# A graph layer beside a normalised node stream: forty node tiles moved from the counting stage to the segment sums

## The reference

```python
edge_index = jnp.stack([src, dst])                    # row = src, col = dst
neighbor_sum = segment_sum(x[col], row, n)            # layer 0
deg = maximum(segment_sum(1, row, n), 1)
mean_neighbor = neighbor_sum / deg
h_mean = (x + mean_neighbor) * 0.5 @ W_mean + b_mean
h_concat = [x @ W_ego + b_ego, mean_neighbor @ W_nb + b_nb]
gate = sigmoid(gate_weight * node_vec + gate_bias)
x = layernorm(x + (1 - gate) * h_mean + gate * h_concat)
...
h = per head: softmax-like weights of edges from two-layer features, segment sums over row   # layer 1
x = layernorm(x + h)
```

## Time and profile before

| | us |
|---|---|
| median of 3 runs (lowest, highest) | 3582.08 (3581.09, 3584.49) |
| the profiled execution, its own time | 3585.29 |
| its span, first to last instruction | 3583.2 |
| mean granted TensorE clock over the span | 0.965 |

### The profile page before, as it was taken

One profiled execution on the slowest core, in us unless ns is written; L12 is line 12 of the kernel. 1 busy time (PEld: TensorE's weight loads), 2 busy tenths in 40 slices (PEclk: granted clock), 3 DMA queues, 4 the chain that ended last, 5 costly groups with the idle time before them and its releaser, 6 DMA issues. The chain is left out here.

```text
span 3583.2 us, 66785 instructions
## 1 busy us (share of the span) xinstructions
PE 3161.0 (88%) x15901; PEld 2177.7 (61%) x15901; DVE 2730.8 (76%) x9307; ACT 1892.2 (53%) x4499; POOL 1802.4 (50%) x1831
## 2 busy tenths in 40 slices
PE   4998887885898888499999999999999999995775
PEld 2455555553555555377777777777777777773333
DVE  4999997875333334388888888888888888887997
ACT  3666666663555545244444444444444444443886
POOL 0006675665777775544444444444444444420777
PEclk9999999997999999799999999999999999997998
DMA  4988777863555555433333333333333333322885
GB/s 146 322 312 274 259 259 266 276 214 123 184 170 177 177 183 183 136 124 117 117 117 117 117 116 115 116 115 116 115 115 116 116 116 116 116 80 78 270 270 196
DMA packets 289120, 596.12 MB, mean 166 GB/s; under 512 B 41438, under 2 KB 198922, under 8 KB 289062
## 3 DMA queue, kind: packets, MB, share of 16 engines
q1 hardware_dynamic: 212950, 362.51, 30.1%
q0 software_dynamic: 75744, 232.45, 20.0%
q10 hardware_dynamic: 368, 0.52, 0.0%
HBM read 287.39 MB, written 322.05 MB: 170 GB/s over the span
## 5 line engine op out<-in xcount | busy, mean ns | idle before, releaser
L1027 PE MATMUL bank<-w_node,xT 128*128 128x384 f32 x1564 | 605.5, 511 | 95.3 <-ACT bank L615 94.2
L1216 POOL TENSOR_TENSOR u_hc<-u_hc 128x1536 f32<-128x1536 f32 x98 | 270.2, 2758 | 759.5 <-DVE u_h L1326 735.4
L1438 PE MATMUL bank<-xh,w1h 128*128 128x512 f32 x1568 | 538.8, 425 | 19.1 <-DVE xl L1355 14.3
L1268 ACT ACTIVATE hidT<-bank,b1c 128x512 f32<-128x512 f32 x392 | 268.6, 685 | 536.3 <-PE bank L1438 536.2
L1438 PE MATMUL bank<-xh,w1l 128*128 128x512 f32 x1568 | 495.0, 397 | 0.0
L1438 PE MATMUL bank<-xl,w1h 128*128 128x512 f32 x1568 | 491.8, 395 | 0.0
L1349 DVE TENSOR_SCALAR hidT<-bank,b1c 128x512 f32<-128x512 f32 x392 | 294.3, 751 | 202.9 <-PE bank L1438 199.8
L1027 PEld LDWEIGHTS bank<-w_node,xT 128*128 128x128 f32 x1564 | 287.3, 198 | 264.8 <-ACT bank L615 118.8
L1452 PE MATMUL bank<-hidT,w2f 128*64 128x256 f32 x3136 | 381.7, 385 | 1.5 <-issue 1.5
L615 ACT ACTIVATE bank<-bias_all 128x512 f32<-128x512 f32 x391 | 235.0, 601 | 273.1 <-DVE H L725 267.8
L1364 DVE STREAM_TRANSPOSE feat<-catT 32x256 f32<-32x256 f32 x784 | 342.8, 437 | 17.1 <-ACT catT L1277 3.0
(11 more groups left out here) (273 smaller groups left out, 6612.9 us busy)
## 6 DMA issues: line engine op xcount, KB each, us to landing
hc_tab<-H SPq DMA_DIRECT2D x78, 960.0 KB
hc_tab<-zero_row SPq DMA_DIRECT2D x26, 2880.0 KB
er<-edge_tab SPq DMA_DIRECT2D x98, 512.0 KB, 4.4
X<-in_x SPq DMA_DIRECT2D x78, 640.0 KB
out_x<-O SPq DMA_DIRECT2D x78, 640.0 KB
edge_tab<-u_x SPq DMA_DIRECT2D x98, 256.0 KB, 2.2
edge_tab<-feat SPq DMA_DIRECT2D x98, 256.0 KB, 2.2
u_hc<-hc_tab,u_idx POOLq DMA_INDIRECT x392, 4.3
```

The costliest lines, as they stand in the source:

```text
L1027: ins = t_.matmul(p[:, 0:384], xT[i % XR][:, c * P:(c + 1) * P], w_node[:, c, :], start=False, stop=c == 1, skip_group_check=True)
L1216: g.tensor_tensor(c, c, u_hc[s][:, :, MULT:MULT + 3].unsqueeze(3).to_broadcast([P, 4, 3, P]), ALU.mult).then_inc(u_scaled, 1)
L1268: a.activation(hidT[m][:, :], bank[2 + m % 2][:, :], ACT.Relu, bias=b1c[:, m:m + 1])\
L1438: ins = t_.matmul(bank[2 + m % 2][:, :], w[:, c, m * P:(m + 1) * P], xx[s][:, c, :], start=n == 0, stop=n == 5)
```

## The change

Counting handles 48 edge tiles in a round of ten node tiles, and the segment sums handle 16, where both handled 24. Counting so ends 40 node tiles earlier, everything up to the sums moves forward by 40 tiles, and the sums take 40 node tiles more. With it: the one-hot ring is 12 deep instead of 8 in use, `RS` is 16, one PSUM bank holds the transposes of the sums and four hold their products (two and three before), a semaphore counts the gathers of two neighbouring buffers, and the clears are 15 of 26 node tiles instead of 26 of 15.

```diff
-        e_idx = sb("e_idx", [P, 24, 4], I32)
+        e_idx = sb("e_idx", [P, 32, 4], I32)
-        ZT = 15
+        ZT = 26
-        oh = tmp("oh", [P, TEN, 2 * DIG], F16)
+        CR = 12
+        oh = tmp("oh", [P, CR, 2 * DIG], F16)
-        RS = 12
+        RS = 16
-        xg_in = [sem(f"xg_in{q}") for q in range(RS)]
-        cn_out = [sem(f"cn_out{q}") for q in range(RS)]
+        xg_in = [sem(f"xg_in{q}") for q in range(RS // 2)]
+        cn_out = [sem(f"cn_out{q}") for q in range(RS // 2)]
-        CNT, FIRST, SORT1, SORT2, TABLES, SUMS, FIX = 0, 83, 85, 189, 291, 293, 378
-        AT = [0, 2, 4, 7, 9, 12, 14, 16, 19, 21]
-        TURNS, PRODS = (3, 4), (5, 6, 7)
-        LOOPS = ((2, 8), (10, 18), (20, 28), (30, 37))
+        CNT, FIRST, SORT1, SORT2, TABLES, SUMS, FIX = 0, 43, 45, 149, 251, 253, 379
+        PER = {CNT: 4 * CR, SUMS: RS}
+        AT = {begin: [many * w // TEN for w in range(TEN + 1)] for begin, many in PER.items()}
+        TURN, PRODS = 3, (4, 5, 6, 7)
+        LOOPS = ((2, 4), (6, 14), (16, 24), (27, 37))
-        def tiles24(j, i, begin, late=0):
+        def tiles_of(j, i, begin, late=0):
             r, w = run(j, i, begin + late)
-            for k in range(AT[w], AT[w + 1] if w + 1 < TEN else 24):
-                t = r * 24 + k
+            for k in range(AT[begin][w], AT[begin][w + 1]):
+                t = r * PER[begin] + k
...
                     if after(t, 2 * RS):
-                        for r in range(RS):
-                            pool.wait_ge(cn_out[r], (n * 2 + q // RS - 1) * 16)
+                        for r in range(RS // 2):
+                            pool.wait_ge(cn_out[r], (n * 2 + q // RS - 1) * 32)
...
                 def run_sum(t, q, n):
-                    dve.wait_ge(xg_in[q], n * 16 + 16)
+                    dve.wait_ge(xg_in[q // 2], n * 32 + 32)
...
                 def turn_sum(t, q):
                     pe.wait_ge(acc_ready, t + 1)
-                    if after(t, 2):
-                        pe.wait_ge(turned_out, t - 1)
+                    if after(t, 1):
+                        pe.wait_ge(turned_out, t)
...
                 def product_sum(t, q):
                     pe.wait_ge(turned_out, t + 1)
-                    if after(t, 3):
-                        pe.wait_ge(cn_ready, t - 2)
+                    if after(t, 4):
+                        pe.wait_ge(cn_ready, t - 3)
```

More of the change, by code:

```diff
@@ L587, in put @@
                                          in_=cn[q % RS][:, :], in_offset=None, bounds_check=last_half, oob_is_err=False)\
-                        .then_inc(cn_out[q % RS], 16)
+                        .then_inc(cn_out[q % RS // 2], 16)
                 ringed(pool, ET, 2 * RS, [(put, 10), (index, 0), (fetch, 0)])
-                for q in range(RS):
-                    pool.wait_ge(cn_out[q], SLOTS[q] * 16)
+                for r in range(RS // 2):
+                    pool.wait_ge(cn_out[r], (SLOTS[2 * r] + SLOTS[2 * r + 1]) * 16)
                 g.dma_start(head_c[:, :], hc_tab[N:N + P, 0, :]).then_inc(head_in, 16)
@@ L642, in copy_sum @@
                         act.wait_ge(prod_ready, t - 3)
-                    a.activation(accT[q % 4][:, :], bank[TURNS[q % 2]][:, 0:D], ACT.Copy).then_inc(turned_out, 1)
+                    a.activation(accT[q % 4][:, :], bank[TURN][:, 0:D], ACT.Copy).then_inc(turned_out, 1)
                 def main_part(t, q, n):
@@ L647, in main_part @@
                     if after(t, RS):
-                        act.wait_ge(cn_out[q], n * 16)
-                    a.activation(cn[q][:, :], bank[PRODS[q % 3]][:, 0:U], ACT.Copy, scale=row_b[:, bass.ds(t, 1)])\
+                        act.wait_ge(cn_out[q // 2], n * 32)
+                    a.activation(cn[q][:, :], bank[PRODS[q % 4]][:, 0:U], ACT.Copy, scale=row_b[:, bass.ds(t, 1)])\
                         .then_inc(cn_ready, 1)
@@ L663, in side @@
                     if part == 3 or now is not None and SUMS < now:
-                        for t, k, r in tiles24(j, i, SUMS, 1):
+                        for t, k, r in tiles_of(j, i, SUMS, 1):
                             if not isinstance(t, int) or t <= ET + 2:
@@ L752, in count_tile @@
                 def count_tile(t, q):
-                    if after(t, 8):
-                        dve.wait_ge(oh_used, t - 7)
+                    if after(t, CR):
+                        dve.wait_ge(oh_used, t - (CR - 1))
                     for d in range(2):
@@ L951, in side @@
                     if part == 0 or now is not None and now < FIRST:
-                        for t, k, r in tiles24(j, i, CNT):
+                        for t, k, r in tiles_of(j, i, CNT):
                             if not isinstance(t, int) or t < ET:
-                                count_tile(t, k % 8)
+                                count_tile(t, k % CR)
                     if now == FIRST:
@@ L965, in side @@
                     if part == 3 or now is not None and SUMS <= now:
-                        for t, k, r in tiles24(j, i, SUMS):
+                        for t, k, r in tiles_of(j, i, SUMS):
                             if not isinstance(t, int) or t < ET:
-                                run_sum(t, k % RS, r * 2 + k // RS)
+                                run_sum(t, k % RS, r + k // RS)
                     if now is not None and now - FIX in (0, 2, 5):
@@ L1075, in turn_sum @@
                     pe.wait_ge(acc_ready, t + 1)
-                    if after(t, 2):
-                        pe.wait_ge(turned_out, t - 1)
+                    if after(t, 1):
+                        pe.wait_ge(turned_out, t)
                     for c in range(2):
-                        ins = t_.transpose(bank[TURNS[q % 2]][:, c * P:(c + 1) * P], acc[q][:, c * P:(c + 1) * P],
+                        ins = t_.transpose(bank[TURN][:, c * P:(c + 1) * P], acc[q][:, c * P:(c + 1) * P],
                                            ident[:, :])
@@ L1120, in side @@
                     if part == 0 or now is not None and 1 <= now < FIRST:
-                        for t, k, r in tiles24(j, i, CNT, 1):
+                        for t, k, r in tiles_of(j, i, CNT, 1):
                             if not isinstance(t, int) or t < ET:
-                                count_tile(t, k % 8)
+                                count_tile(t, k % CR)
                     for k, begin in enumerate((SORT1, SORT2)):
@@ L1545, in build @@
         zo_out = cn_out[0:SL]
-        IN0 = [len(range(q, ET, RS)) * 16 for q in range(SL)]
+        IN0 = [(len(range(2 * q, ET, RS)) + len(range(2 * q + 1, ET, RS))) * 16 for q in range(SL)]
         pair_rows = edge_tab.rearrange("b p d -> (b p) d")
```

6 lines of the change are left out of this document (3 added, 3 removed).

## The result

| | us |
|---|---|
| before, median of 3 runs | 3582.08 |
| after, median of 3 runs (lowest, highest) | 3546.27 (3545.29, 3547.38) |
| ratio, 95% interval | 0.9901 [0.9887, 0.9914] |
| the profiled execution after, its own time and its span | 3545.29, 3543.6 |

The change makes the kernel 35.8 us faster. Forecast was 60 us, 3522. The time lies in the range, 3511 to 3552, but outside the likeliest case's own range, which ended at 3532: it is rival A, the DMA queue in the first sorting pass, at some two fifths of its full size.

What follows compares the result with a forecast made beforehand. VectorE was taken to bound counting, GpSimd's issue the sorting passes and sums. Counting -57.2, refreshes -3.8, tail -2.1 and clears +3 sum to -60.1 us, giving 3522 us against the median; range 3511 to 3552.

Steps and rivals of the forecast that it cites:

- likeliest case: Whole kernel: the summed terms hold, 3522 us, own range 3511 to 3532 us; chance 0.62.
- rival A: First sorting pass: the DMA queue bounds it, up to 47 us lost; 3532 to 3566 us; chance 0.17.
- Counting, -57.2: Counting stage, paced by VectorE: 40 node tiles' own work of 1.43 us each leaves its path, 57.2 us less.
- The clears in the first pass, +3: First sorting pass: longer clears delay X's second load in ten rounds; bounds 0 and 47 us, 3 us taken.
- the lead: End of first sorting pass: VectorE is 8.6 us ahead of GpSimd and may lose about that before anything later moves.
- The moved tiles in the sums, 0: Segment sums: 40 more node tiles cost nothing beside GpSimd's issue; 60 us if that cover were gone.
- refreshes -3.8: Segment sums: rings of 16 cut GpSimd's index refreshes from 17 to 13, 0.94 us each, 3.8 us less.
- tail -2.1: After the last sum: 16 node tiles follow instead of 17, 2.1 us less.
- The cover: Segment sums: GpSimd's issue time hides node tiles, 3.93 us of TensorE per tile against 4.25 us of GpSimd.
- B: Rival: TensorE bounds the segment sums, 534 us against GpSimd's 521; 3535 to 3553 us; chance 0.13.
- C: Rival, slower: TensorE's mean granted clock under 0.82 stretches the sums to 590 us; 3589 us and more; chance 0.04.
- D: Rival, no gain: VectorE's node work holds back GpSimd's issue in the sums, 57 us; 3579 us; chance 0.04.

Runs made afterwards that it cites:

- two later profiles: Changed kernel run once more, 3544.09 us, and changed kernel with clears of 10 node tiles instead of 26, 3527.29 us; kernel before beside them 3582.01 us.
- first three groups: Changed kernel, variants of its clears or gather semaphores, and kernel before with clears of 26; the kernel before beside them took 3912.96, 3852.35 and 3926.49 us.

## Why the prediction was right and where it failed

**Counting, -57.2, measured -62.2.** The mechanism was right, and a wait was overlooked. The compares cost the same 0.196 us (ten in 1.95 us below); the node part of a tile became cheaper, (134.2 - 392 x 0.197) / 43 = 1.33 us, with 134.2 from tile 0 to tile 43, where I took 1.43 from before. In the timeline four compares start at 150.88. The node tile behind them, of before, with TensorE's product that it reads; and then a run of compares after, with the node tile behind it:

```profile
151.91 0.48 DVE L718 SCALAR_TENSOR_TENSOR H<-bank,gates,X 128x256 f32<-128x256 f32 x1 [0.17 <-issue]
```

```profile
150.13 1.52 PE L1027 MATMUL bank<-w_node,xT 128*128 128x384 f32 x4
```

```profile
119.81 2.04 DVE L758 TENSOR_SCALAR oh<-iota_d,dig 128x256 f16<-128x256 f16 x10
121.76 0.47 DVE L720 SCALAR_TENSOR_TENSOR H<-bank,gates,X 128x256 f32<-128x256 f32 x1
```

After four compares the node tile starts 151.91 - 150.88 = 1.03 us after the first of them, 0.24 more than 4 x 0.197; after ten, 121.76 - 119.81 = 1.95 us, nothing is lost. The product ends at 150.13 + 1.52 = 151.65, 0.26 us before the node tile starts. So VectorE had waited for TensorE, though the row puts the idle time down to "issue". Over the whole of counting before, 25 node tiles start late behind their compares, by 6.0 us in all, and for each of them TensorE's product had ended 0.26 us or less before; where the product was there 0.7 us or more ahead, nothing is lost, behind runs of four compares too. After the change there is one such tile, 0.1 us. "The timeline of VectorE shows no idle time in it" was therefore not so, and TensorE, busy for 45.2 of 48 us in the earlier trace rows, was a second limit of counting. My sum left the 43 tiles that stay their share of the 6.0, some 3.1 of the 5.0 us that the gain is larger; the rest I did not trace. My low bound of the gain, 53.6 us from 0.215 a compare, had put the wait on the wrong side: it belongs to the node tile.

**The clears in the first pass, +3, measured +17.7, and +2.5 behind it.** This is the step that failed: "22.6 + 5.6 x 1.06 = 28.5 of 29.0: it fits, and hardly", and then, of 0 and 47, "the lower end: 3 us taken". The order of events was right, down to the transfer that would be late (X's second load of the round, behind the clear), and so was its landing: 25.4 us after the first load's issue by my reckoning, ready at 26.5 in the round above. What was wrong is when the tile was wanted. I put it at four node tiles of 2.9 us after the load's issue, 11.6, "no earlier than that"; it was wanted (276.63 + 1.46 = 278.09) 9.0 us after it. The trace of before had it so already. Of the 391 pairs of transposes on line 1019, that of tile 125 is this one, 361.45 - 352.01 = 9.4 us after the load's issue:

```profile
361.45 0.38 PE L1019 MATMUL bank<-ident,X 128*128 128x128 f32 x2
```

With it in place of 363.6, my own landing at 363.5 was 2 us late in every round, some 20 us in ten, before the lead is taken off. SyncE's 4.00 us in the issue of the O store, which I had costed at nothing, added little: in the round above the X load was issued 1.22 us after VectorE's last read of its buffer had started (267.88), where 0.75 is usual. That is 0.5 us late; it was 1.9 us at most, and under 0.2 from the fourth of the ten rounds on. Nothing of this was a surprise of rate. The DMA engines were busy for 0.93 of rounds of (510.5 - 193.1) / 10.4 = 30.5 us, 28.4 us, where I had forecast 28.5 of 29.0. A queue that is full to 98% in order, with a deadline in its midst, has hardly any room; the lower end of the bounds was the wrong end to choose, and the empty stretch in the earlier trace rows, 361 to 364, was not spare time ahead of the deadline at 361.45. The lead of 8.6 us took only part: the 104 tiles from 45 to 149 took 317.4 us (289.9 before), 27.5 more, of which 7.3 did not reach the second pass.

**The second pass and the stretch behind it, 0, measured 0.** 287.4 and 18.6 us, against 287.6 and 18.7.

**The moved tiles in the sums, 0; refreshes -3.8; tail -2.1; measured +4.5 and +2.7.** The cover held in the main: 125 node tiles instead of 85, and 4.5 us more (1.7 and 10.0 in the two later profiles). A tile takes (1369.6 - 836.2) / 124 = 4.30 us, forecast were 4.2 to 4.3. GpSimd's steps after (start, duration, what it waited for):

```profile
1123.34 1.02 POOL L588 DMA_INDIRECT hc_tab<-cn,e_idx  x1 [0.30 <-issue]
...
1125.94 1.14 POOL L588 DMA_INDIRECT hc_tab<-cn,e_idx  x1 [0.30 <-issue]
1127.05 0.28 POOL L571 COPY e_idx<-idx_s 128x64 int32 x1
...
1129.46 1.02 POOL L588 DMA_INDIRECT hc_tab<-cn,e_idx  x1 [0.30 <-issue]
```

2.60 us a step, and 3.52 with a refresh, as before. (My count of "sixteen gaps" at 32.1 us left out the last three gathers, 7.8 us, and took the first twelve at full price, where they took 24.4, with no scatters beside most of them: two errors that cancel.) Of the 8.3 us between 510.9 and 519.2, 5.6 sit in three of the groups of 16 edge tiles, which took 43.9, 45.0 and 44.2 us where the others take 42.5. GpSimd's scatters wait for ScalarE's product in this stage, 7.3 us from 880 to 1330, and upstream VectorE waits for a pair of gathers, here one of the longer waits:

```profile
1201.16 0.48 DVE L947 SCALAR_TENSOR_TENSOR acc<-acc,same,xg 128x256 f32<-128x256 f32 x1
1207.30 0.48 DVE L947 SCALAR_TENSOR_TENSOR acc<-acc,same,xg 128x256 f32<-128x256 f32 x1 [5.66 <-DMA xg<-in_x,e_idx]
```

That the one makes the other late is argued, not shown: the longest such wait before was 6.3 us, with single semaphores, and the runs that undo the pairing fell where VectorE did not wait for gathers. Whether the pairing, the single transpose bank or TensorE's thinner slack (3.93 of 4.25 us) costs these microseconds stays open. Two transpose banks were not run.

One of my signs against the cover did come: VectorE's waits in the sums turned from gathers to TensorE. Before (880 to 1390 us), and after (880 to 1330):

```profile
DVE acc L945 <- DMA xg<-in_x,e_idx: 239.5, 115, 6.3
...
DVE H L718 <- PE bank L1027: 47.5, 29, 3.7
```

```profile
DVE H L720 <- PE bank L1029: 106.3, 73, 3.2
...
DVE acc L947 <- DMA xg<-in_x,e_idx: 99.0, 44, 6.8
```

So TensorE is close behind GpSimd in this stage now, at 94% busy, and the stage grew by a few microseconds only.

The rule of the Trainium skill on the port that VectorE and GpSimd share ("SBUF — State Buffer", section "SBUF: two separate sides"), which I had set against the cover, does not show here either: VectorE is busy for 50% of the sums instead of 39%, and a scatter with its gather takes the same 2.60 us. The rule is about VectorE's two-port operations; whether any of this stage is one, no trace here tells.

**The rivals.** A came, at 17.7 to 20.2 of 47 us; I gave it 0.17 and the forecast 0.62, and with the tile's time read from the trace it should have had the larger share. That the total lies within the range owes something to the range being wide enough to hold half of A, and to counting's 5.0 us more. B did not come: TensorE's clock was 0.98 in the sums and the stage 519 us, where B wanted 534 and more, though its sign in VectorE's waits did. That its low clock follows waits held. C and D did not come: no stage is under 0.95, and the steps are 2.60 us. In the first three groups something of B's kind did decide, as VectorE's waits for TensorE in the sums show, and the changed kernel kept a gain of 0.2% there, which its interval doesn't tell from none.

**What follows the last node tile** is 4.4 us shorter, and the change doesn't touch it. The profiled execution of before lay 3.2 us above its median, and I had taken these off; whether they lay here nothing shows.

## What to carry to other kernels

When bytes are moved in time within an in-order queue, sum the bytes in front of the next transfer that somebody waits for, and compare that with its deadline; the mean share of the DMA engines over the round doesn't answer it. Read the deadline from the row of the instruction that reads the data, not from a number of tiles times a mean: here the row stood 2 us earlier than the mean had it. A filler transfer that nobody waits for can be cut and spread: here pieces of 10 tiles, two in a round, instead of 26 in one, were worth 16.8 us, nearly half as much again as the change they belong to. And work that is moved under another engine's issue is free only as long as that engine paces the stage: the sums grew by 2 to 10 us where GpSimd did, and by 44 in the runs in which much else was slow.

## What the runs showed of the hardware

The issue of an O store of 0.66 MB on SyncE took 2.95 to 4.16 us behind a 5.1 MB clear in the ten rounds with a wait, and 7.56 behind the last clear; behind clears of 2.9 MB (before) and 2.0 MB it took 0.33 to 0.34 in the same pass. So a long transfer in the queue can hold up the engine that issues behind it. That the queue was full is my reading; the trace shows the times alone.

The same kernel took 3926.49 us on one chip and, on the same chip in a later group of runs, 3582.01, with all runs of a group agreeing. The longer ones show waits whose releaser is not on the core, and their TensorE stages stretch while VectorE's counting takes the same time. What disturbs them no trace here shows.
